# Transposes of the finished rows three steps behind their normalisation instead of one, in a graph network's second gather stage

## The chip, the cores and the metric

One NeuronCore of a Trainium2 chip runs the whole program. The metric is the device time of one execution in microseconds; the kernel before takes 3145.21 us as the median of three runs (3142.08 to 3146.8). "GpSimd" is POOL in the rows, "VectorE" DVE, "ScalarE" ACT, "TensorE" PE (PEld its weight loads), and "SyncE" SP; a q behind a name is that engine's sequencer or queue.

## The reference

Two layers of a graph network over 6250 nodes of 256 features and 100000 edges that are sorted by their destination. The part around the change is the second layer's message passing and linear attention:

```python
xn = _layernorm(x, axis=-1)
x = x + _L1_gnn_ref(xn, ...) + _L1_mix_ref(xn[None], ...)[0]
x = x + _L1_ffn_ref(_layernorm(x, axis=-1)[None], ...)[0]

# in _L1_gnn_ref
src = node_in[edge_src]
...
msg_rad = h @ fc_w2 / np.float32(np.sqrt(64.0))
messages = msg_ang * msg_rad
agg = jax.ops.segment_sum(messages, edge_dst, num_segments=node_in.shape[0])
```

The x after the second line is called x3 in the kernel; its layer norm, f3, is the input of the last feed-forward layer. That layer chooses its two experts for all rows at once, from the mean of f3 over the nodes.

## The kernel before, in words

The program is a row of phases; phase "g2" is the second gather stage, from about 1700 to 2735 us of the execution. Its time is laid out in steps by `timeline`: each engine has a list of plans, a plan being the steps at which the items of a kind begin and, for each function on them, how many steps later it runs. Each engine issues its instructions in the order of the steps and, in one step, in the order of the plans. A step is only an order and takes no time of its own; semaphores (`Steps`, `Landing`) make an engine wait for the others.

- **Groups** (`GROUPS`, 391 of them, one a step). A group is 2 x 128 edges. At its step GpSimd gathers their source rows from DRAM with two indirect DMAs (`gather`, L2484), into a buffer of 13 groups. One step later VectorE builds the one-hot matrix of destinations and half of its weighted copies (`make_hot`, L598 and L2119), three steps later ScalarE the other half (`weigh`, L2533). Five steps later TensorE sums the messages by destination (`sums`, L2131) into one of four PSUM banks, and seven steps later VectorE adds the bank to a ring of sums in SBUF (`accumulate`, L2614). The place in the ring is data, so ahead of each addition VectorE's sequencer loads it into a register (L2606).
- **Tiles** (`P9`, 50 tiles of 125 nodes, their steps at least 3 apart, in the last third of the stage). SyncE loads the tile's transposed rows xmT (L2459) and its x2 (L2463) at its step. VectorE adds the bias to x2 three steps later (`add_bias`, L2669); four steps later TensorE multiplies the rows and the finished ring columns with the weights (`product`, L2773 and L2778); five steps later VectorE adds up x3 (`x3_of`, L2677 and L2679) and takes its row statistics (L1442 to L1448). SyncE stores x3 at six steps (L2467). ScalarE clears ring columns for a later tile once a product has read them (`zero`, L2497).
- **Finished rows** (`F3`, for each pair of tiles 12 and 15 steps after the pair's second). VectorE normalises x3 to f3 (`f3_of`, L1457); SyncE stores it one step later (L2471). TensorE transposes it (`turned`, L2785) into the single bank TURN, ScalarE copies the transpose out to f3T, with the sums over nodes that the last layer needs (`copy`, L2524), and SyncE stores f3T (L2475). f3 and f3T have four buffers each.
- **Radial weights** (`RAD`, `CHUNKS`) for the edges are made along the way: L2715 and L2727 on TensorE, L2545 on ScalarE, L2589 and L2595 on VectorE.

In TensorE's order of one step the sums come first, then the radial work, then `turned`, then `product`. The tile's functions with the waits that tie the two engines are these:

```python
def product(i):
    ...
    sums3.wait(e, i - 1, "x3")
def turned(i):
    ln.norm.wait(e, i, "f")
    copied.wait(e, i - 1, "c1")
def x3_of(i):
    r = i % XR
    rows.wait(e, i, "rows")
```

Of the kernel before, what the change touches and what calls it, by code (L numbers as in the profile page):

```python
# [136 lines left out]
def gps_kernel(nc, A, out):  # L137
# [55 lines left out]
    with top:  # L193
# [2109 lines left out]
        with Phase("g2") as ph:  # L2303
# [121 lines left out]
            with nc.Block() as block:  # L2425
                @block.sync
                def _(e):
                    for to, src in ((rel[:, :, :].rearrange("p g j -> p (g j)"), rel_d), (base[:, :], base_d)):
                        e.dma_start(to, src).then_inc(s_in, 16)
                    def load_emb(n):  # L2430
                        eturn.wait(e, NV * (n - 1) - 1, "turn")
                        load_chunk(e, emb, n, e_in)
                    load_emb(1)
                    e.dma_start(w2r[:, :], A["L1_gnn_fc_w2"].rearrange("c a -> (a c)").partition_broadcast(P)).then_inc(s_w2r, 16)
                    e.dma_start(wkv[:, :, :], chunked(A["L1_mix_WkvT"])).then_inc(s_w, 16)
                    e.wait_ge(s_wz, 1)
                    for u in range(UU):
                        e.dma_start(w1b[u * K1:(u + 1) * K1, u, :], A["L1_gnn_fc_w1"]).then_inc(s_wb, 16)

                    def load_kv(i):  # L2440
                        proj.wait(e, i - 2, "v")
                        k_in.start(e.dma_start(kT[:, i % 2, :, :],
                                               xmT_d[i // 2].rearrange("p (c t n) -> p c t n", c=DC, t=2)[:, :, i % 2, :]),
                                   i % 2)

                    off = e.value_load(own_row[0:1, 0:1], min_val=0, max_val=N)

                    def load_rest(i):
                        e.dma_start(wq[:, :, :], chunked(A["L1_mix_Wq"])).then_inc(s_c, 16)
                        e.dma_start(wo[:, :, :], chunked(A["L1_mix_WoutT"])).then_inc(s_c, 16)  # L2450
                        e.dma_start(f3[:, 0, :], A["L1_mix_bout"].partition_broadcast(TN)).then_inc(s_c, 16)
                        e.dma_start(rwt[:, :, :], chunked(A["L1_ffn_Wr"])).then_inc(s_head, 16)
                        e.dma_start(br[:, :], A["L1_ffn_br"].rearrange("(a n) -> a n", a=1)).then_inc(s_head, 16)

                    def load(i):
                        if i == 0:
                            dots.wait(e, NT - 1, "dots")
                        rows.wait(e, i - XI, "rows")
                        x_in.start(e.dma_start(xmT[:, i % XI, :, :],  # L2459
                                               xmT_d[i // 2].rearrange("p (c t n) -> p c t n", c=DC, t=2)[:, :, i % 2, :]),  # L2460
                                   i % XI)
                        biased.wait(e, i - XI, "xb")
                        x_in.start(e.dma_start(x2[:, i % XI, :], xm_d[ds(off + i * TN, TN), :]), i % XI)  # L2463

                    def store_x3(i):
                        sums3.wait(e, i, "x3")
                        x_out.start(e.dma_start(tile_of(x3_d, i), x3[:, i % XR, :]), i % XR)  # L2467

                    def store_f3(i):
                        ln.norm.wait(e, i, "f")  # L2470
                        f_out.start(e.dma_start(tile_of(f3_d, i), f3[:, i % FR, :]), i % FR)  # L2471

                    def store_f3T(i):
                        copied.wait(e, i, "c1")
                        t_out.start(e.dma_start(f3T_d[i], f3T[:, i % FR, :, :].rearrange("p c n -> p (c n)")), i % FR)  # L2475
                    timeline(LAST_STEP, (CHUNKS[:-1], [(lambda i: load_emb(i + 2), 2)]), (KV, [(load_kv, 0)]), ([FIRST], [(load_rest, 0)]),
                             (P9, [(load, 0), (store_x3, 6)]), (F3, [(store_f3, 1), (store_f3T, 4)]))
                @block.gpsimd
                def _(e):
                    def gather(g):  # L2480
# [9 lines left out]
                @block.scalar  # L2490
                def _(e):
                    def zero(b):
                        rows.wait(e, b - RB, "rows")
                        to = ring[:, :, cols(b)]
                        pads = [ring[:, :, RING1:RING1 + WIN]] if b % RB == 0 else []
                        for part in (*pads, to):
                            ins = e.activation(part, iota[:, 0:1].unsqueeze(2).broadcast_to([P, SL, part.shape[2]]), ACT.Copy)  # L2497
                        blank.done(ins, "zero")

                    def square(i):  # L2500
                        sizes.wait(e, i - 1, "sum")
                        dots.wait(e, i - 2, "dots")
                        for q, bank, to, name, copy in ((0, KB, k1, "k", "raw"), (H1, V, v1, "v", "copy")):
                            proj.wait(e, i, name)
                            squares.done(e.activation(sq[:, q:q + H1, :].rearrange("p h d -> p (h d)"), ps[0:TN, bank, :],
                                                      ACT.Square), name)
                            squares.done(e.activation(to[:, i % 2, :], ps[0:TN, bank, :], ACT.Copy), copy)

                    def roots(i):
                        sizes.wait(e, i, "prod")  # L2510
                        kn.wait(e, i - 2, "k")
                        kroot.done(e.activation(rs[:, i % 2, :], pr[:, i % 2, :], ACT.Sqrt), "root")

                    def deviations(i):
                        ln.stats.wait(e, 2 * i + 1, "pre")
                        ln.norm.wait(e, 2 * i + 1 - XR, "f")
                        at = slice(2 * i % XR, 2 * i % XR + 2)
                        spread_of.done(e.activation(ln.rs[:, at, 0], ln.pre[:, at, 0], ACT.Sqrt), "dev")

                    def copy(i):  # L2520
                        turn.wait(e, i, "turn")
                        t_out.wait(e, i % FR, i // FR - 1)
                        for c in range(DC):
                            copied.done(e.activation(f3T[:, i % FR, c, :], ps[:, TURN, c * TN:(c + 1) * TN], ACT.Copy,  # L2524
                                                     accum_out=fsum[:, c, i:i + 1]), f"c{c}")
                    def weigh(g):
                        u, n, k = g % HR, g // (P // 2), 2 * g % P + 1
                        ready.wait(e, g, "hot")
                        scaled.wait(e, n - 1, "wr")
                        summed.wait(e, g - HR, "sums")  # L2530
                        w = WINS[g]
                        for m in range(4):
                            ins = e.activation(hotw[:, u, 1, m * w:(m + 1) * w], hot[:, u, 1, 0:w], ACT.Copy,  # L2533
                                               scale=chunk(n)[:, k, m:m + 1])
                        ready1.done(ins, "hotw")

                    def copy_emb(i):
                        eturn.wait(e, i, "turn")
                        hidden.wait(e, i - 2, "hid")
                        ecopy.done(e.activation(embT[:, i % 2, :], ps[0:UU * K1, 2, 0:P], ACT.Copy), "embT")  # L2540

                    def do_silu(i):
                        hidden.wait(e, i, "hid")
                        rads.wait(e, i - 2, "mul")
                        silu.done(e.activation(hs[:, i % 2, :, :],  # L2545
                                               ps[:, 7, 0:UU * C1].rearrange("p (u c) -> p u c", u=UU),
                                               ACT.Silu, scale=K1 ** -0.5), "silu")
                    timeline(LAST_STEP, (GROUPS, [(weigh, 3)]), (RAD, [(do_silu, 7), (copy_emb, 3)]), (ZERO, [(zero, 0)]),
                             (KV, [(square, 5), (roots, 8)]), (PAIRS, [(deviations, 9)]), (F3, [(copy, 2)]))

                @block.vector
                def _(e):
# [147 lines left out]
                def _(e):  # L2700
# [80 lines left out]
# [3 lines that stand above are left out]
                        for c in range(DC):  # L2784
# [1 line left out]
                                             ident[0:TN, 0:TN])  # L2786
                        turn.done(mm, "turn")
                    timeline(LAST_STEP, (GROUPS, [(sums, LEAD)]), (RAD, [(hidden_of, 5), (turn_emb, 1)]), (CHUNKS, [(turn_radial, 11)]),
                             (KV, [(products, 11), (project, 3)]), (MIX, [(mix_wo, 1), (mix_wq, 3)]), (F3, [(turned, 1)]),
                             (P9, [(product, 4)]))  # L2790


# [263 lines left out]
```

## Time and profile before

| | |
|---|---|
| median of 3 runs | 3145.21 us (3142.08 to 3146.8) |
| the profiled execution | 3143.74 us |
| its span | 3142.1 us |
| mean granted TensorE clock | 0.942 of full speed |
| TensorE busy, matmuls | 2647.7 us (84%) |
| VectorE busy | 1739.7 us (55%) |
| ScalarE busy | 1429.4 us (45%) |
| GpSimd busy | 1809.6 us (58%) |

The profile is of one execution. Its span is what lies between the first and the last instruction. A busy share over the whole span says little of this stage: each phase has another limit, and the sequencer's own instructions (register loads, semaphores, the issue of a DMA) count as idle time. The row of a wait names the instruction that waited and the one whose end released it.

### The profile page before, as it was taken

To read this page: it belongs to the slowest core of one execution; us is meant where nothing else is said; L and a number is where in the kernel's file an instruction comes from. 1 tells how busy PE (TensorE), PEld (TensorE's weight loads), DVE (VectorE), ACT (ScalarE), POOL (GpSimd) and SP (SyncE) were. 2 spreads that over 40 slices of the span, in tenths; PEclk is the share of its full clock that TensorE was granted. 3 is DMA by queue.
4 is the path that set the end of the run, shared out by engine and by line. 5 is a ranking of instruction groups with operands and counts; after the bars stand their busy time and mean duration, and the time that the engine had idled before them with its cause. 6 is when DMAs were issued, how large, how long until landed. Compare 5 with 4: busy or idle time off the path is not lost. (4 is left out here: it accounts for less than half of the span.)

```text
span 3142.1 us, 54187 instructions
## 1 busy us (share of the span) xinstructions
PE 2647.7 (84%) x14909; PEld 2219.0 (71%) x14909; DVE 1739.7 (55%) x5390; ACT 1429.4 (45%) x3996; POOL 1809.6 (58%) x1962
## 2 busy tenths in 40 slices
PE   1999998898988998699933899999887888689998
PEld 1877778777887886688832666666676677578886
DVE  7733336787776567333355556566566667533333
ACT  4022222442222553233346988788566766322221
POOL 5777777767773355344476777777777777200000
PEclk9999999999999998899965999999999999899999
DMA  7364446667673774333367444444466655422222
GB/s 224 113 190 144 136 140 200 222 198 219 216 220 123 215 237 146 103 95 95 92 186 233 116 125 117 125 117 128 121 181 177 176 162 161 123 76 72 70 65 55
DMA packets 291700, 464.77 MB, mean 148 GB/s; under 512 B 91221, under 2 KB 224276, under 8 KB 290074
## 3 DMA queue, kind: packets, MB, share of 16 engines
q1 hardware_dynamic: 207804, 232.37, 25.2%
q0 software_dynamic: 81216, 221.98, 24.0%
q10 hardware_dynamic: 2402, 7.19, 0.7%
q8 instruction: 115, 1.88, 0.2%
q14 instruction: 163, 1.34, 0.1%
HBM read 349.16 MB, written 112.23 MB: 147 GB/s over the span
## 5 line engine op out<-in xcount | busy, mean ns | idle before, releaser
L2484 POOL DMA_INDIRECT g_got<-xm_d,idx x782 | 757.4, 969 | 253.6 <-issue 219.4
L876 POOL DMA_INDIRECT g_got<-xn_d,idx x702 | 680.4, 969 | 240.5 <-issue 211.3
L2131 PEld LDWEIGHTS ps<-g_hotw,g_got 128*128 128x128 f32 x3128 | 402.3, 196 | 161.6 <-issue 81.3
L2131 PE MATMUL ps<-g_hotw,g_got 128*128 128x128 f32 (+11 forms) x3128 | 423.0, 285 | 91.0 <-DMA g_got<-xm_d,idx 59.9
L1261 PEld LDWEIGHTS ps<-g_hot,g_got 128*128 128x128 f32 x2808 | 357.5, 196 | 80.4 <-DMA g_got<-xn_d,idx 37.7
L1261 PE MATMUL ps<-g_hot,g_got 128*128 128x120 f32 (+4 forms) x2808 | 372.2, 280 | 36.4 <-DMA g_got<-xn_d,idx 25.7
L2533 ACT ACTIVATE g_hotw<-g_hot,g_wr 128x16 f32<-128x16 f32 (+8 forms) x1308 | 300.8, 309 | 90.8 <-DVE g_hot L598 90.2
L1453 POOL TENSOR_TENSOR p_ln_rs<-p_ln_pre,neg_half 125x2 f32<-125x2 f32 x50 | 35.2, 704 | 518.2 <-DVE p_ln_pre L1448 518.2
L2614 DVE TENSOR_TENSOR g_ring<-g_ring,ps 128x84 f32 (+10 forms) x391 | 133.4, 341 | 305.9 <-PE ps L2131 155.8
L2047 POOL DMA_INDIRECT z_d<-p_yj,p_to x108 | 121.9, 1128 | 205.1 <-DVE p_to L2080 183.3
L2934 ACT ACTIVATE p_hid<-ps,p_b 128x250 f32<-128x250 f32 x200 | 82.9, 466 | 278.6 <-PE ps L2896 278.6
L2011 PE MATMUL ps<-gin_hid,p_wj 128*128 128x256 f32 x864 | 197.4, 382 | 1.1 <-ACT gin_hid L1953 0.8
L1662 PE MATMUL ps<-gin_w,gin_hid 128*125 128x256 f32 x800 | 190.4, 388 | 9.1 <-POOL p_before L1721 9.1
L2913 PE MATMUL ps<-p_w,p_hid 128*125 128x256 f32 x800 | 179.2, 382 | 22.2 <-ACT p_hid L2934 22.2
L1393 PE MATMUL ps<-g_hT,g_w 128*128 128x250 f32 x800 | 191.9, 384 | 0.8 <-DVE g_hT L1084 0.8
L1072 DVE TENSOR_TENSOR g_ring<-g_ring,ps 128x40 f32 (+9 forms) x351 | 74.0, 211 | 208.7 <-PE ps L1261 125.7
L2896 PE MATMUL ps<-p_f3T,p_w 128*128 128x250 f32 x800 | 175.3, 375 | 13.3 <-DMA p_w<-in_L_ffn_W 13.3
L2913 PEld LDWEIGHTS ps<-p_w,p_hid 128*125 128x125 f32 x800 | 148.2, 188 | 52.9 <-ACT p_hid L2934 30.2
L2737 PE MATMUL ps<-g_half 128*125 128x512 f32 x400 | 184.9, 605 | 0.0
L2011 PEld LDWEIGHTS ps<-gin_hid,p_wj 128*128 128x128 f32 x864 | 165.1, 191 | 24.4 <-issue 1.1
L1962 ACT ACTIVATE gin_hid<-ps,p_wj 128x256 f32<-128x256 f32 x216 | 90.7, 471 | 188.6 <-PE ps L2011 188.6
L2896 PEld LDWEIGHTS ps<-p_f3T,p_w 128*128 128x128 f32 x800 | 151.6, 190 | 33.1 <-issue 13.4
(376 smaller groups left out, 5042.3 us busy)
## 6 DMA issues: line engine op xcount, KB each, us to landing
h_d<-gin_hid SPq DMA_DIRECT2D x23, 1000.0 KB, 7.8
gin_hid<-h_d SPq DMA_DIRECT2D x23, 1000.0 KB
p_xr<-jobs_d SPq DMA_DIRECT2D x54, 258.0 KB, 2.9
g_got<-xm_d,idx POOLq DMA_INDIRECT x782
g_half<-xmT_d SPq DMA_DIRECT2D x100, 125.0 KB
g_got<-xn_d,idx POOLq DMA_INDIRECT x702
p_wj<-z_d SPq DMA_DIRECT2D x50, 224.0 KB
q_d<-g_qo SPq DMA_DIRECT2D x25, 250.0 KB
```

The source lines that it names most:

```text
L876: landed.start(e.indirect_dma_start(got[:, k % (2 * GB), :], None, xn_d[0:N, :], bass.IndirectOffsetOnAxis(ap=idx[:, HT + k:HT + k + 1], a ...
L1261: mm = e.matmul(to, got[:, 2 * (g % GB) + j, c * P:(c + 1) * P], hot[:, g % HR, j, 0:w].unsqueeze(1).broadcast_to([P, r, w]), start=(j == ...
L1393: mm = e.matmul(ps[:, 5 + n % 2, k * BN:(k + 1) * BN], w1[:, c, f:f + P], hT[:, i % 2, c, :], start=(c == 0), stop=(c == DC - 1))
L1662: mm = e.matmul(ps[0:TN, i % 2, t * D:(t + 1) * D], hid[:, slot(i), c, t * TN:(t + 1) * TN], w2[:, c, :], start=(c == 0), stop=(c == HC - 1))
L2011: mm = e.matmul(ps[:, 2 * k + u, o * JOB:(o + 1) * JOB], w[:, c, o * P:(o + 1) * P], src[:, u, c, :], start=(c == 0), stop=(c == DC - 1))
L2131: mm = e.matmul(to, rows[j][:, c * P:(c + 1) * P], hotw[:, j, c * w:4 * w].unsqueeze(1).broadcast_to([P, r, n]), start=(j == 0), stop=(j = ...
L2484: landed.start(e.indirect_dma_start(got[:, 2 * (g % GB) + j, :], None, xm_d[0:N, :], bass.IndirectOffsetOnAxis(ap=idx[:, 2 * g + j:2 * g + ...
L2533: ins = e.activation(hotw[:, u, 1, m * w:(m + 1) * w], hot[:, u, 1, 0:w], ACT.Copy, scale=chunk(n)[:, k, m:m + 1])
L2614: added.done(e.tensor_tensor(to, to, sums_of(bank_of(g)[0], w, bank_of(g)[1]), ALU.add), "add")
L2737: mm = e.matmul(ps[0:TN, bank, :], kT[:, i % 2, c, :], wkv[:, c, at:at + INNER], start=(c == 0), stop=(c == DC - 1))
L2896: mm = e.matmul(ps[:, q, m * BN:(m + 1) * BN], w1[:, k, c, f * P:(f + 1) * P], f3T[:, u, :, c * TN:(c + 1) * TN], start=(c == 0), stop=(c ...
L2913: mm = e.matmul(ps[0:TN, 4 + u, t * D:(t + 1) * D], hid[:, u, k, f, t * TN:(t + 1) * TN], w2[:, k, f, :], start=(j == 0), stop=(j == 2 * F ...
```

## The change

Three numbers of plans are changed, all on `F3`. TensorE's transposes `turned` go from one to three steps after the normalisation, ScalarE's `copy` from two to four, and SyncE's `store_f3T` from four to six. What they compute and their counts stay.

```diff
@@ SyncE
-                             (P9, [(load, 0), (store_x3, 6)]), (F3, [(store_f3, 1), (store_f3T, 4)]))
+                             (P9, [(load, 0), (store_x3, 6)]), (F3, [(store_f3, 1), (store_f3T, 6)]))
@@ ScalarE
-                             (KV, [(square, 5), (roots, 8)]), (PAIRS, [(deviations, 9)]), (F3, [(copy, 2)]))
+                             (KV, [(square, 5), (roots, 8)]), (PAIRS, [(deviations, 9)]), (F3, [(copy, 4)]))
@@ TensorE
-                             (KV, [(products, 11), (project, 3)]), (MIX, [(mix_wo, 1), (mix_wq, 3)]), (F3, [(turned, 1)]),
+                             (KV, [(products, 11), (project, 3)]), (MIX, [(mix_wo, 1), (mix_wq, 3)]), (F3, [(turned, 3)]),
```

**TensorE, where a tile comes every third step.** The rows are the transposes (L2785), the product (L2773, L2778) and the sums of groups (two rows of L2131 each). Before:

```order
L2785 MATMUL ps<-ident,g_f 128x125 x2
L2773 MATMUL ps<-g_mix,g_half 125x256 x2
L2778 MATMUL ps<-wm,g_ring 125x128 x2
L2778 MATMUL ps<-wm,g_ring 125x64 x2
L2778 MATMUL ps<-wm,g_ring 125x128
L2778 MATMUL ps<-wm,g_ring 125x64 x2
L2131 MATMUL ps<-g_hotw,g_got 128x128 x2
L2131 MATMUL ps<-g_hotw,g_got 128x96 x2
L2131 MATMUL ps<-g_hotw,g_got 128x128 x2
L2131 MATMUL ps<-g_hotw,g_got 128x96 x2
L2131 MATMUL ps<-g_hotw,g_got 128x128 x2
L2131 MATMUL ps<-g_hotw,g_got 128x96 x2
```

Now:

```order
L2785 MATMUL ps<-ident,g_f 128x125 x2
L2131 MATMUL ps<-g_hotw,g_got 128x128 x2
L2131 MATMUL ps<-g_hotw,g_got 128x96 x2
L2727 MATMUL ps<-g_w1b,g_embT 128x512
L2773 MATMUL ps<-g_mix,g_half 125x256 x2
L2778 MATMUL ps<-wm,g_ring 125x128 x2
L2778 MATMUL ps<-wm,g_ring 125x64 x2
L2778 MATMUL ps<-wm,g_ring 125x128
L2778 MATMUL ps<-wm,g_ring 125x64 x2
L2131 MATMUL ps<-g_hotw,g_got 128x128 x2
L2131 MATMUL ps<-g_hotw,g_got 128x96 x2
L2131 MATMUL ps<-g_hotw,g_got 128x128 x2
```

The transposes stood directly ahead of a product; now the sums of one group follow them, and the product comes behind those. Of the 50 products, 30 stand directly behind transposes before, and 3 now.

**TensorE, at the stage's end.** The last sums and the last two products. Before:

```order
L2785 MATMUL ps<-ident,g_f 128x125 x2
L2131 MATMUL ps<-g_hotw,g_got 128x176 x2
L2131 MATMUL ps<-g_hotw,g_got 128x132 x2
L2785 MATMUL ps<-ident,g_f 128x125 x2
L2773 MATMUL ps<-g_mix,g_half 125x256 x2
L2778 MATMUL ps<-wm,g_ring 125x128 x2
L2778 MATMUL ps<-wm,g_ring 125x64 x2
L2778 MATMUL ps<-wm,g_ring 125x128
L2778 MATMUL ps<-wm,g_ring 125x64 x2
L2773 MATMUL ps<-g_mix,g_half 125x256 x2
```

Now:

```order
L2131 MATMUL ps<-g_hotw,g_got 128x176 x2
L2131 MATMUL ps<-g_hotw,g_got 128x132 x2
L2785 MATMUL ps<-ident,g_f 128x125 x2
L2773 MATMUL ps<-g_mix,g_half 125x256 x2
L2778 MATMUL ps<-wm,g_ring 125x128 x2
L2778 MATMUL ps<-wm,g_ring 125x64 x2
L2778 MATMUL ps<-wm,g_ring 125x128
L2778 MATMUL ps<-wm,g_ring 125x64 x2
L2785 MATMUL ps<-ident,g_f 128x125 x2
L2773 MATMUL ps<-g_mix,g_half 125x256 x2
```

Before, transposes stand directly ahead of the last product but one. Now those are of an earlier tile, and the transposes that stood there come behind that product.

**SyncE, where a tile comes every third step.** The stores are of x3 (x_d, L2467), f3 (f_d, L2471) and f3T (L2475), the loads xmT (L2459) and x2 (L2463). Before:

```order
L2471 DMA f_d<-g_f 125x256
L2475 DMA f3T_d<-g_f3T 128x250
L2459 DMA g_half<-xmT_d 128x2x125
L2463 ISA
L2463 DMA g_half<-xm_d 125x256
L2467 DMA x_d<-g_half 125x256
L2471 DMA f_d<-g_f 125x256
```

Now:

```order
L2467 DMA x_d<-g_half 125x256
L2475 DMA f3T_d<-g_f3T 128x250
L2471 DMA f_d<-g_f 125x256
L2459 DMA g_half<-xmT_d 128x2x125
L2463 ISA
L2463 DMA g_half<-xm_d 125x256
L2467 DMA x_d<-g_half 125x256
L2475 DMA f3T_d<-g_f3T 128x250
```

The store of f3T went out behind that of the next tile's f3; now it goes out behind that of x3. It stands behind f3's in 37 of 46 rows of SyncE's order before and in 12 of 49 now, and behind x3's in 8 before and 31 now. GpSimd's and VectorE's orders are the same in both kernels. (ISA is a register instruction of SyncE for the address of x2.)

## Rows read from the trace of the kernel before

**Rows 1.** The gathers of L2484: count, duration ns min/median/max, first and last start.
```profile
L2484 POOL DMA_INDIRECT g_got<-xm_d,idx x782: 942/946/2625, 1703.0 to 2697.3; - x196
```

**Rows 2.** Chain, then timeline (start us, us, what): a landing; last gather; last sums.
```profile
2303.15 5.08 DMA g_got<-xm_d,idx
...
2697.29 1.06 POOL L2484 DMA_INDIRECT g_got<-xm_d,idx  x1 [0.30 <-issue]
...
2717.91 1.21 PE L2131 MATMUL ps<-g_hotw,g_got 128*128 128x176 f32 x8
```

**Rows 3.** A stretch, its length, busy us of PE, PEld, DVE, ACT, POOL, clock, DMA.
```profile
2400.00:2500.00 100.00, 80.97 (x534) 69.69 (x532) 67.82 (x209) 70.95 (x239) 75.93 (x80) 0.93 0.63 175
```

**Rows 4.** Waits from 2280 to 2740 us: us in total, times, longest.
```profile
DVE g_ring L2614 <- issue: 80.9, 104, 2.0
...
PE ps L2785 <- DVE g_f L1457: 49.8, 33, 3.2
...
DVE g_half L2677 <- PE ps L2778: 13.8, 11, 2.5
```

**Rows 5.** VectorE's sequencer loads, 1900 to 2200, then 2300 to 2700 us.
```profile
L2606 DVEq TENSOR_LOAD <-g_base x119: 297/303/321, 1899.9 to 2198.9; - x119
...
L2606 DVEq TENSOR_LOAD <-g_base x150: 298/315/1705, 2300.9 to 2697.1; - x150
```

**Rows 6.** Timeline of one cycle, 2359 to 2367 us; in brackets the idle time before.
```profile
2359.02 0.15 DVE L1448 TENSOR_SCALAR g_ln_pre<-g_ln_mv 125x1 f32<-125x1 f32 x1
...
2361.13 0.39 DVE L2614 TENSOR_TENSOR g_ring<-g_ring,ps 128x224 f32 x1 [1.96 <-issue]
...
2362.09 0.41 DVE L1457 TENSOR_SCALAR g_f<-g_half,g_ln_mv,g_ln_rs 125x256 f32<-125x256 f32 x1
...
2362.55 0.68 PE L2785 MATMUL ps<-ident,g_f 125*128 125x125 f32 x2 [3.07 <-DVE g_f L1457]
...
2362.83 0.36 SPq L2475 DMA_DIRECT2D f3T_d<-g_f3T  x1
...
2363.59 0.29 DVE L2119 TENSOR_TENSOR g_hotw<-g_hot,g_wr 128x128 f32<-128x128 f32 x1
...
2365.57 0.39 DVE L2614 TENSOR_TENSOR g_ring<-g_ring,ps 128x224 f32 x1 [1.68 <-issue]
...
2366.94 0.28 DVE L2677 SCALAR_TENSOR_TENSOR g_half<-ps,xm_mv,g_half 125x64 f32<-125x64 f32 x1 [0.52 <-PE ps L2778]
```

**Rows 7.** Timeline of the stage's end, from 2721 us.
```profile
2721.30 0.43 PE L2785 MATMUL ps<-ident,g_f 125*128 125x125 f32 x2 [2.18 <-DVE g_f L1457]
...
2724.11 0.28 DVE L2677 SCALAR_TENSOR_TENSOR g_half<-ps,xm_mv,g_half 125x64 f32<-125x64 f32 x1 [2.09 <-PE ps L2778]
...
2727.49 0.28 DVE L2677 SCALAR_TENSOR_TENSOR g_half<-ps,xm_mv,g_half 125x64 f32<-125x64 f32 x1 [0.85 <-PE ps L2778]
```

**Rows 8.** VectorE's waits from 2300 to 2700 us.
```profile
DVE g_half L2677 <- PE ps L2778: 8.8, 7, 2.5
```

**Rows 9.** Timeline, 2308 to 2316 us: late data, then the longest wait of L2677.
```profile
2308.27 2.00 PE L2131 MATMUL ps<-g_hotw,g_got 128*128 128x112 f32 x8 [2.12 <-DMA g_got<-xm_d,idx]
...
2315.96 0.28 DVE L2677 SCALAR_TENSOR_TENSOR g_half<-ps,xm_mv,g_half 125x64 f32<-125x64 f32 x1 [2.47 <-PE ps L2778]
```

**Rows 10.** Timeline from 2542 us: a burst behind f3 without f3T.
```profile
2542.08 0.33 DVE L2119 TENSOR_TENSOR g_hotw<-g_hot,g_wr 128x160 f32<-128x160 f32 x1
...
2543.44 0.45 DVE L2614 TENSOR_TENSOR g_ring<-g_ring,ps 128x280 f32 x1 [0.65 <-issue]
```

**Rows 11.** Timeline from 2647 us: f3T's store between x3's and the next load.
```profile
2647.22 0.26 SPq L2467 DMA_DIRECT2D x_d<-g_half  x1
...
2647.52 0.36 SPq L2475 DMA_DIRECT2D f3T_d<-g_f3T  x1
...
2648.01 0.15 DVE L1448 TENSOR_SCALAR g_ln_pre<-g_ln_mv 125x1 f32<-125x1 f32 x1
...
2649.34 0.48 DVE L2614 TENSOR_TENSOR g_ring<-g_ring,ps 128x308 f32 x1 [1.17 <-issue]
```

## The prediction

> **What bounds the kernel now.** The edit lives in the second gather stage, so I first look at who paces it. The gathers of L2484 run from 1703.0 to 2697.3 us, 782 of them [rows 1]: (2697.3 - 1703.0) / 781 = 1.27 us each, two to a step, so 2.55 us a step. GpSimd's idle time is the short gap it takes between any two, so up to 2697 the gathers set the pace. But the stage does not end with them. The last gather starts at 2697.29 and takes 1.06 us; a gather's data reaches TensorE 5.08 us after it where nothing is behind; that would be 2703.4, yet the sums of the last group start at 2717.91 [rows 2]. So 14.5 us of backlog stand behind the gathers at their end, and whatever holds TensorE and VectorE back while the rows are finished (2280 to 2740 us) is paid there.
>
> Next, which of the two engines made the backlog. In 100 us of that stretch TensorE is busy 80.97 and VectorE 67.82 [rows 3], which points to TensorE. The waits say the reverse. TensorE waited 49.8 us in 33 pieces for the normalised rows f3 of VectorE (L2785 behind L1457); VectorE waited for finished products only 13.8 us in 11 pieces (L2677 behind L2778), and its other idle time, 80.9 us ahead of the ring additions of L2614, has "issue" as its end [rows 4]. That issue time is VectorE's own sequencer, which reads the ring position of a group by a load (L2606) ahead of each addition. In the quiet part of the stage that load never takes over 321 ns; here it takes up to 1705 [rows 5]. So VectorE with its sequencer is the chain, TensorE is the one that waits, and **the 49.8 us are not for sale**: a wait taken from TensorE is worth what it takes from VectorE's waits.
>
> **The tie between them** is seen in one cycle [rows 6]. VectorE makes f3 of one tile at 2362.09; TensorE has stood 3.07 us for it, turns it at 2362.55, and only then runs the product of the newest tile (before: 30 of the 50 products stand right behind a transpose in TensorE's order; after: 3). The product is done as VectorE's L2677 starts at 2366.94, after a wait of 0.52 us. From the transposes to L2677 are 4.39 us; for the same work at the stage's end they are 2724.11 - 2721.30 = 2.81 [rows 7], so the stop was followed by a slow stretch. The mean granted clock around it is 0.93 [rows 3]: part of the time stands at 1.2 instead of 2.4 GHz.
>
> **The change, term by term**, against the profiled execution (3143.74 us; the median of the runs, 3145.21, stands 1.5 above it). Nothing is added or removed. VectorE's and GpSimd's orders are the same, row for row.
>
> *Transposes three steps behind.* TensorE reaches the transposes two steps later, some 5 us at 2.55 a step; the longest stop it has now is 3.2 us [rows 4], so f3 is there. The product of that step no longer has the f3 stop, nor the transposes, ahead of it. How much of VectorE's wait goes:
> - 2300 to 2700: 8.8 us in 7 waits [rows 8]. The largest, 2.47 us at 2315.96, was not made by f3: TensorE had stood 2.12 us for gathered data at 2308.27 [rows 9], and will again. I leave it in; the other six are 8.8 - 2.47 = 6.3 us, all behind products that a transpose precedes. Gain 6.3 (bounds 3 and 8.8).
> - after 2700: 13.8 - 8.8 = 5.0 us. Of these, 0.85 us is the last product's, which starts on the row sums of the product before it and keeps its wait. The wait of 2.09 us at 2724.11 goes: TensorE stood 2.18 us for f3 until 2721.30 ahead of that product, though the last sums were done at 2719.1 (2717.91 + 1.21) [rows 7]. It comes behind the last gather, so it counts one for one. The other 5.0 - 0.85 - 2.09 = 2.1 us likewise. Gain 4.2 (bounds 2 and 4.2).
>
> *What replaces the stop.* Freed, TensorE runs ahead until the next sums need a bank whose addition VectorE has not done: four banks, additions seven steps behind their gather against five for the sums, so it can be two steps ahead and not more. It will stand there; nobody waits for it then. Its earlier sums free gather buffers earlier, which gathers that run back to back do not need. Cost 0.
>
> *Copies on ScalarE, two steps later*: 100 copies, unchanged, still one step behind their transposes. The buffer is four tiles deep and a tile comes at most every third step, so a slot is copied into again 12 steps on at the earliest; its store follows the copy by two steps, as before, and 10 steps are left for it to land. Cost 0.
>
> *Stores of f3T on SyncE, two steps later.* SyncE's queue is in order. Now the store goes out right behind the store of the next f3 (37 of the 46 rows of it in SyncE's order), followed by the loads; afterwards mostly right behind the store of x3 (31 of 49 rows), and in 12 behind f3. This matters for the long loads of L2606. In the cycle shown, f3T's store goes at 2362.83, and from the row at 2363.59 to the ring addition at 2365.57 are 1.98 us [rows 6]. Where the burst held no f3T, the same two rows are 2543.44 - 2542.08 = 1.36 apart [rows 10]: 0.62 less. Behind row statistics the store of x3 alone gave 2361.13 - 2359.02 = 2.11 [rows 6], x3 with f3T 2649.34 - 2648.01 = 1.33 [rows 11], so an f3T there costs nothing that these rows show. For 37 - 12 = 25 tiles: between 25 x 0.62 = 15.5 us gained and, were the second place to answer as the first does, nothing. That loads wait for transfers at all is my reading of a coincidence, and the same kinds of burst differ by 0.8 us, so I take a third of the way to the gain: 4.5 us.
>
> *Tail.* The last four transposes stand behind the last product in both orders: 0.
>
> Sum: 6.3 + 4.2 + 4.5 = 15.0 us. Of it 6.3 + 2.1 + 4.5 = 12.9 fall before the last sums, within the 14.5 us of backlog; all of the backlog and the 2.09 at the end would be 16.6. So 3143.7 - 15.0 = 3128.7 on the profiled run, 3130.2 as a median. **I predict 3130 us.** Without the load term, 3134.7; with everything at its upper bound the cap of the backlog gives 3128.6.
>
> **Rivals.**
> *A, VectorE's waits come back.* If TensorE only stops elsewhere, and its products still end late, the gain shrinks to 0 to 4 us. For it: all of TensorE's idle time remains, since VectorE sets the pace, and it is now taken at the bank waits. Against it: a product then starts two VectorE steps, some 5 us, ahead of its reader, and even at 4.39 us it is done. Time: 3142 to 3145. The Trainium skill (TensorE: Matmul & The Clock Gate, the part on the HAM clock gate) has a rule on this side: an array that stood idle runs at half its clock until it has been busy again. By that rule moving a stop does not cure a slow stretch, and where one stop of 3 us becomes a longer one it makes more of them; the 4.39 against 2.81 us above agree with it.
>
> *B, slower: the second burst.* The f3T store joins x3's, just ahead of the load that follows the row statistics, and there is such a load for every tile. That load is on the chain. If it always went from the short case to the long one of my rows (1.33 to 2.11, 0.78 us), half of that as a mean over the 50 tiles is 19.5 us; with 10.5 gained and no relief behind f3: 3145.2 + 9.0 = 3154. It decides from 10.5 / 50 = 0.21 us per tile on. Against it: the two rows stand the wrong way round for it.
>
> *C, TensorE was the bound after all*: busy share 81%. Then the 49.8 us pull away all backlog there is: 14.5 + 2.1 = 16.6, so 3128.6 as a median. Against it: VectorE's waits for it are a quarter of the reverse.
>
> **How the numbers follow.** No change here means within 0.2%, 6.3 us, which is about what a measurement of this kernel can tell apart. Forecast 0.68, C 0.08, A 0.18, B 0.06. The forecast's own range is 3125 to 3138: both waits at their bounds, the load term from 0 to the cap, 2 us of scatter between runs. To hold 8 in 10 it must reach into A: 3123 to 3142. Faster: the forecast nearly whole (below 3138.9), C, and little of A: 0.78. Same: most of A, the end of the forecast, a part of B: 0.17. Slower by over 6.3 us: 0.05.
>
> **What would show it.** Right: in the new profile TensorE's wait at L2785 falls from 49.8 us to under 10, and TensorE waits by tens of us more at L2131 behind L2614; L2677's 13.8 us fall to some 4 (2.5 and 0.85 stay); idle time "issue" ahead of L2614 falls by some 4; gathers still end near 2697, and the last sums come at about 2705 instead of 2717.9. Wrong: L2677's waits as large as before (A), "issue" ahead of L2614 grown by 10 us or more (B), or a last gather later than 2699, which I have no term for.

## The result and the profile after

The changed kernel takes 3131.71 us as the median of five runs (3124.7 to 3144.05), against 3145.21 (3142.08 to 3146.8) before. The ratio is 0.9963, with a 95% interval of 0.9947 to 0.9979: by this ratio it is 11.6 us faster (between 6.6 and 16.7; the two medians lie 13.5 apart), a small gain that is clear of the noise. Its runs lie 19 us apart, more than the first ones of the kernel before; its profiled execution took 3133.81 us.

The page of the changed kernel, its span and the first line of part 1 (busy us, share, instructions):

```profile
span 3132.2 us, 54187 instructions
...
PE 2653.0 (85%) x14909; PEld 2221.0 (71%) x14909; DVE 1737.8 (55%) x5390; ACT 1430.2 (46%) x3996; POOL 1815.6 (58%) x1962
```

TensorE's busy time is 2653.0 us, and was 2647.7: nothing was saved on it. The gathers of the stage (columns as in [rows 1]):

```profile
L2484 POOL DMA_INDIRECT g_got<-xm_d,idx x782: 942/946/2247, 1705.4 to 2702.9; - x196
```

They begin 2.4 us later than in [rows 1] and end 5.6 us later, at 1.277 us each instead of 1.273. The edit touches neither the work ahead of the stage nor the gathers' own instructions. In the traces of before, this kernel and three of the experiments below (all but same_step of those on chip 9), the 782 gathers take 994.3 to 1000.5 us from the first start to the last, 994.6 in two_steps, which is half of this change. So this profiled run lost some 3 us to the pace of its gathers, for which the forecast had no term; whether the edit has a part in it is not shown.

The waits of the changed kernel from 2280 to 2740 us (us in total, times, longest), to be held against [rows 4]:

```profile
DVE g_ring L2614 <- issue: 76.0, 105, 2.2
...
DVE g_ring L2614 <- PE ps L2131: 30.9, 33, 1.6
PE ps L2131 <- DVE g_ring L2614: 30.6, 23, 3.0
PE ps L2131 <- DVE g_hot L598: 25.0, 26, 3.4
ACT g_ring L2497 <- PE ps L2778: 23.0, 15, 3.2
...
DVE g_half L2677 <- PE ps L2778: 5.3, 3, 3.0
...
PE ps L2785 <- DVE g_f L1457: 2.3, 1, 2.3
```

TensorE's wait for f3, 49.8 us, is down to 2.3 (one wait, in the tail). In its place stand 30.6 us for ring additions (15.0 before) and 25.0 for one-hot matrices (8.6 before), both made by VectorE. Most of TensorE's idle time is still there, in other places: from 2280 us to the end of its last sums it is idle 71.9 us of 432.0, where it was 80.1 of 439.1. VectorE's wait for products fell from 13.8 us to 5.3. ScalarE, whose clearing of ring columns also waits for products, shows the same, with 23.0 us where it had 65.5.

The timeline of one cycle, answering to [rows 6] (start, us, line, and in brackets the idle time before):

```profile
2362.84 0.41 DVE L1457 TENSOR_SCALAR g_f<-g_half,g_ln_mv,g_ln_rs 125x256 f32<-125x256 f32 x1
...
2364.28 1.10 PE L2131 MATMUL ps<-g_hotw,g_got 128*128 128x128 f32 x8 [0.76 <-DVE g_hot L598]
...
2365.22 0.38 PE L2785 MATMUL ps<-ident,g_f 125*128 125x125 f32 x2
...
2366.66 0.28 DVE L2677 SCALAR_TENSOR_TENSOR g_half<-ps,xm_mv,g_half 125x64 f32<-125x64 f32 x1
...
2367.47 1.04 PE L2773 MATMUL ps<-g_mix,g_half 128*125 128x256 f32 x4
...
2368.35 1.64 PE L2778 MATMUL ps<-wm,g_ring 128*125 128x128 f32 x14
...
2370.37 0.41 DVE L1457 TENSOR_SCALAR g_f<-g_half,g_ln_mv,g_ln_rs 125x256 f32<-125x256 f32 x1
```

f3 is made at 2362.84. TensorE does not wait for it: it sums a group, then turns at 2365.22. VectorE reads the finished product of the tile before at 2366.66 with no idle time, and TensorE starts the next product (L2773) at 2367.47, before VectorE has even made the next f3 (2370.37). From one f3 to the next are 7.5 us here.

The end of the stage, answering to [rows 2] and [rows 7]:

```profile
2702.87 0.96 POOL L2484 DMA_INDIRECT g_got<-xm_d,idx  x1 [0.30 <-issue]
...
2709.65 2.31 PE L2131 MATMUL ps<-g_hotw,g_got 128*128 128x176 f32 x16
...
2711.80 0.38 PE L2785 MATMUL ps<-ident,g_f 125*128 125x125 f32 x2
...
2712.01 1.03 PE L2773 MATMUL ps<-g_mix,g_half 128*125 128x256 f32 x4
...
2714.56 0.43 PE L2785 MATMUL ps<-ident,g_f 125*128 125x125 f32 x2
...
2715.20 0.28 DVE L2677 SCALAR_TENSOR_TENSOR g_half<-ps,xm_mv,g_half 125x64 f32<-125x64 f32 x1
...
2716.01 1.13 PE L2773 MATMUL ps<-g_mix,g_half 128*125 128x256 f32 x4 [1.01 <-DMA g_half<-xm_d]
...
2718.65 0.28 DVE L2677 SCALAR_TENSOR_TENSOR g_half<-ps,xm_mv,g_half 125x64 f32<-125x64 f32 x1 [0.92 <-PE ps L2778]
```

The last sums (two groups in one row) end at 2711.96, 9.1 us after the start of the last gather; before, they ended at 2719.12, 21.8 us after it. The backlog is 12.7 us shorter. Since the gathers took 3.2 us longer, the stretch from the first gather's start to the end of the last sums is shorter by less: 1006.6 us against 1016.1, 9.5 us. I call this stretch the stage's length below. The last product but one (2712.01) has a transpose of 0.38 us ahead of it and no stop, and its reader at 2715.20 has no idle time where 2.09 us stood. The last reader waits 0.92 us (0.85 before), and its product now 1.01 us for its loaded rows, a small new wait.

The sequencer's loads from 2300 to 2700 us, as in [rows 5]:

```profile
L2606 DVEq TENSOR_LOAD <-g_base x154: 299/318/1964, 2300.7 to 2699.4; - x154
```

Median and longest did not fall: 318 and 1964 ns against 315 and 1705.

### The profile page after: what moved, and what is told of

It is laid out like the page before. It is cut to its first block and busy times, and to the rows that moved or that the text cites. A ratio compares the mean times of both kernels' runs of the same rounds, so it can differ in the third digit from the quotient of the medians.

```text
span 3132.2 us, 54187 instructions
## 1 busy us (share of the span) xinstructions
PE 2653.0 (85%) x14909; PEld 2221.0 (71%) x14909; DVE 1737.8 (55%) x5390; ACT 1430.2 (46%) x3996; POOL 1815.6 (58%) x1962
## 5 line engine op out<-in xcount | busy, mean ns | idle before, releaser
L2484 POOL DMA_INDIRECT g_got<-xm_d,idx x782 | 760.5, 973 | 253.4 <-issue 221.8
L2131 PEld LDWEIGHTS ps<-g_hotw,g_got 128*128 128x128 f32 x3128 | 406.7, 198 | 199.8 <-issue 117.8
L2131 PE MATMUL ps<-g_hotw,g_got 128*128 128x128 f32 (+11 forms) x3128 | 432.7, 288 | 125.0 <-DMA g_got<-xm_d,idx 62.2
L2614 DVE TENSOR_TENSOR g_ring<-g_ring,ps 128x84 f32 (+10 forms) x391 | 133.5, 341 | 303.6 <-PE ps L2131 155.3
L2896 PEld LDWEIGHTS ps<-p_f3T,p_w 128*128 128x128 f32 x800 | 151.3, 189 | 32.2 <-issue 12.5
```

What stands on the lines that cost most here:

```text
L2131: mm = e.matmul(to, rows[j][:, c * P:(c + 1) * P], hotw[:, j, c * w:4 * w].unsqueeze(1).broadcast_to([P, r, n]), start=(j == 0), stop=(j = ...
L2484: landed.start(e.indirect_dma_start(got[:, 2 * (g % GB) + j, :], None, xm_d[0:N, :], bass.IndirectOffsetOnAxis(ap=idx[:, 2 * g + j:2 * g + ...
L2614: added.done(e.tensor_tensor(to, to, sums_of(bank_of(g)[0], w, bank_of(g)[1]), ALU.add), "add")
L2896: mm = e.matmul(ps[:, q, m * BN:(m + 1) * BN], w1[:, k, c, f * P:(f + 1) * P], f3T[:, u, :, c * TN:(c + 1) * TN], start=(c == 0), stop=(c ...
```

## The experiments

Two theories were set against each other. **The tie**: VectorE with its sequencer is the chain of this part of the stage, and the change gains what VectorE had to wait for products that stood behind the f3 stop. **The stores**: the gain is in SyncE's order, through the sequencer's loads. Nine kernels ran, three of them on two chips and the changed one again, on three chips. Chips 14 and 4 ran every kernel some 13% slower than the chip of the result (before: 3560.07 and 3562.46 us), so only ratios to the kernel before on the same chip are compared. No trace of the kernel before was taken there; waits are held against those of store_late.

### The changed kernel again (chip 14)

> The changed kernel itself, for the scale of the others. If the gain of 0.37% stands, 3126 to 3140 us. Theory of the tie (VectorE waited for products that stood behind the f3 stop): L2677's wait from 2280 to 2740 us is again near 5 us where it was 13.8, and the last sums come before 2713 us. Rival of the stores (the gain is in SyncE's order and the sequencer loads L2606): L2677's wait may be anything, and the longest loads behind f3 are shorter. If runs differ by several us, as the first five did, the gathers' own pace should show it: a last gather between 2697 and 2704 us.

3550.13 us, ratio 0.9969 (0.9952 to 0.9987). The ratio stands on a second chip; the expected microseconds do not, since the whole chip was slower. One sign of it is seen in its timeline:

```profile
2717.81 0.27 PE L2785 MATMUL ps<-ident,g_f 125*128 125x125 f32 x1 [1.09 <-issue]
...
2718.53 0.27 PE L2785 MATMUL ps<-ident,g_f 125*128 125x125 f32 x1 [0.45 <-issue]
...
2719.36 0.28 DVE L2677 SCALAR_TENSOR_TENSOR g_half<-ps,xm_mv,g_half 125x64 f32<-125x64 f32 x1 [5.03 <-remote]
```

The two transposes of one tile, one row of two in the timelines above, are 0.72 us apart, with idle time "issue" between them though neither waits for anything, and VectorE then stands 5.03 us for the product; the profile names the releaser "remote". On these chips TensorE itself is often late, so VectorE's waits for products are larger (76.4 us "remote" and 6.8 for TensorE, where some 5 were expected) and partly of another kind. The mean granted clock in the traces of chips 14 and 4 is 0.893 to 0.905, against 0.941 here.

The limit of the stage is another one there too. Its gathers stood idle, in all and by releaser (us, times):

```profile
  PE ps L2131: 127.5, 68
  DMA g_own<-xn_d: 110.0, 48
```

In the trace of the result the first of these was 16.2 us and the second did not occur. The 782 gathers take 1198.6 us here, 1.53 us each. So on chips 14 and 4 the gathers do not set the pace, and their ratios say which edits bring the gain, but not that VectorE is the chain.

### Only the store later (chips 14 and 4)

```diff
-(F3, [(store_f3, 1), (store_f3T, 4)])
+(F3, [(store_f3, 1), (store_f3T, 6)])
```

> Only SyncE's store of f3T goes two steps later; transposes and copies stay where they were. Theory of the tie: nothing that TensorE or VectorE wait for changes, L2677's wait stays at 12 to 15 us, and the time is that of before within 3 us (3142 to 3148). Rival of the stores: at least half of the gain is here, 3135 to 3140 us, with the idle time (issue) ahead of L2614 down by 5 us or more from 80.9.

> Again only the store of f3T two steps later, since the first chip ran all kernels 13% slower, with late instructions on TensorE. Theory of the tie: within 0.1% of before, L2677's wait near 13.8 us. Rival of the stores, now from its row: the burst behind f3 is shorter and idle time (issue) ahead of L2614 falls by 4 us or more, ratio 0.998 to 0.9985.

Ratios 1.0004 (0.9986 to 1.0021) and 1.0007 (0.9989 to 1.0025): no gain, twice. The stops of TensorE at L2785, matmuls and weight loads added up, and below them those of VectorE at L2677, on chip 14 (us, times):

```profile
  DVE g_f L1457: 78.7, 39
  issue: 51.4, 39
```

```profile
  remote: 58.7, 22
  PE ps L2778: 31.5, 15
```

The expected 12 to 15 us at L2677 do not hold on these chips: the two rows make 90.2 us here and 101.2 on chip 4.

### Transposes and copies later, the store in its old place (chips 14 and 4)

```diff
-(F3, [(copy, 2)])
+(F3, [(copy, 4)])
-(F3, [(turned, 1)])
+(F3, [(turned, 3)])
```

> Transposes and copies go two steps later as in the change, the store of f3T stays four steps behind the normalisation, in the step of its copy. Theory of the tie: all of the gain, 3128 to 3138 us, L2677's wait near 5 us, and the burst of stores behind f3 as before the change. Rival of the stores: 3140 to 3146 us. Rival of a stopped queue: SyncE waits for the copy with the next tile's loads behind it; then TensorE waits at L2773 for xmT and the time is above 3146 us.

> Again transposes and copies late, the store in its old place. Theory of the tie: ratio 0.9955 to 0.9975, as the whole change, L2677's wait 4 to 8 us. If the stores brought part of the change's gain, this has less than the change.

Ratios 0.9961 (0.994 to 0.9981) and 0.9967 (0.9952 to 0.9982), the whole gain both times. VectorE's idle time at L2677, chip 14:

```profile
  remote: 77.5, 25
  PE ps L2778: 3.7, 3
```

Together 81.2 us against 90.2 with only the store moved; what is named as TensorE's product fell from 31.5 to 3.7. On chip 4 the sum is 62.2 us against 101.2, where 4 to 8 were expected. The named part fell as the theory says, but the sum does not follow the gain: it fell by 9.0 us on one chip and 39.0 on the other, for nearly the same ratio. SyncE's queue was not stopped to any effect.

### The product ahead of the transposes in a step (chips 14 and 4)

```diff
-(MIX, [(mix_wo, 1), (mix_wq, 3)]), (F3, [(turned, 1)]),
-(P9, [(product, 4)]))
+(MIX, [(mix_wo, 1), (mix_wq, 3)]),
+(P9, [(product, 4)]), (F3, [(turned, 1)]))
```

> The kernel before with one edit: in TensorE's order of a step the product comes ahead of the transposes; the transposes still stand one step behind the normalisation. Theory of the tie in its narrow form (what cost time was the product behind the f3 stop, not the stop): the f3 wait stays at 30 us or more, L2677's wait falls to 3 to 7 us, and the time is 3130 to 3139 us. Wide form (each stop of TensorE costs, since it holds up sums as well): less than half of the gain, 3139 to 3145 us. Rival of the stores: 3142 to 3147.

> Again the kernel before with the product ahead of the transposes in a step. It had three quarters of the gain on the slow chip. Narrow theory: 0.9965 to 0.998, L2677's wait 4 to 8 us, while TensorE still waits over 25 us for f3, which then costs next to nothing. Wide theory: 0.998 to 1.0.

Ratios 0.9976 (0.9959 to 0.9994) and 0.997 (0.9953 to 0.9987). Nothing is moved to another step; two plans have changed places. The stops at L2785 and those at L2677, chip 14:

```profile
  DVE g_f L1457: 27.9, 27
  issue: 9.9, 11
```

```profile
  remote: 80.9, 24
  PE ps L2778: 7.7, 5
```

Most of the gain (0.24% where the whole change and its variant had 0.31 and 0.39% on chip 14, 0.30% beside 0.33% on chip 4) is had by the order inside a step alone. The expected sign of the narrow form did not come, though: TensorE's matmuls at L2785 were to wait 30 us or more for f3 (over 25 on chip 4), and they waited 11.2 and 5.6 us, where store_late had 34.5 and 42.1, since TensorE comes to f3 later by a product. VectorE's stops at L2677 make 88.6 us in all, against 90.2, of which the part named as TensorE's product fell from 31.5 to 7.7. So this edit took away the product behind the stop and most of the stop as well, and on a chip where TensorE holds the gathers back it cannot tell the narrow form from the wide one. Whether the remainder to the full change is real, the intervals do not say.

### Half the dose, and the other way (chip 9)

> Transposes two steps behind the normalisation instead of one, copies three, stores of f3T five: half of the change. Theory of the tie: what counts is that a product no longer stands directly behind a transpose that waits for f3, and that TensorE may be two steps ahead of VectorE anyway; both are had at two steps, so the whole gain of the change is here (ratio to the kernel before 0.996 to 0.998, L2677's wait as small as in the change). Rival of dose (each step of slack frees some of TensorE's stops): half of it, 0.998 to 0.999.

> The other way: transposes in the very step of the normalisation, copies one step later, stores of f3T three. The suspected cost doubled. Theory of the tie: TensorE may now not pass the step that VectorE is in, each product and each group's sums behind a transpose are later by up to a step, L2677's wait grows to twice that of before or more, and the time rises by 0.3 to 1.5%. Rival of the stores, or that TensorE's stops cost nothing: within 0.1% of before.

`turned`, `copy` and `store_f3T` at 2, 3 and 5 give 0.9968 (0.9954 to 0.9981) with a median of 3136.41 us; at 0, 1 and 3 they give 1.0144 (1.0124 to 1.0164), 3194.47 us. This chip ran the kernel before in 3145.29 us, so its microseconds compare with those of the result. The waits of two_steps from 2280 to 2740 us:

```profile
DVE g_half L2677 <- PE ps L2778: 8.2, 5, 3.4
...
PE ps L2785 <- DVE g_f L1457: 2.9, 4, 1.8
```

and those of same_step from 2280 to 2780 us:

```profile
PE ps L2785 <- DVE g_f L1457: 95.4, 40, 5.2
...
DVE g_half L2677 <- PE ps L2778: 73.8, 39, 4.0
POOL g_got L2484 <- PE ps L2131: 54.4, 56, 3.8
```

Two steps bring the gain of three within the intervals: half of the gain would be about 0.9982, just outside the interval, so the dose rival (0.998 to 0.999) is all but excluded. The stage's length says the same: 1006.9 us, against 1006.6 with the whole change. With the transposes in the step of the normalisation VectorE's wait for products is 73.8 us instead of 13.8, 60.0 more, TensorE's wait for f3 is 45.6 us more, and the kernel is 49 us slower; the stage's length is 1065.8 us, 49.7 more. The backlog now reached the gathers themselves, which stood 54.4 us for free buffers (11.9 before) and take 1034.7 us from first to last, 40.4 more. Both waits grew by about what the time did, so this run shows that the tie costs time, not which of the two waits the time follows.

### The ring position loaded early (chip 9)

```diff
+places = {}
+
+def place_of(g):
+    return e.value_load(base[0:1, g:g + 1], min_val=0, max_val=RING1 - 1)
 def accumulate(g):
-    at = e.value_load(base[0:1, g:g + 1], min_val=0, max_val=RING1 - 1)
+    at = places.pop(g) if g in places else place_of(g)
...
     added.done(e.tensor_tensor(to, to, sums_of(bank_of(g)[0], w, bank_of(g)[1]), ALU.add), "add")
+    if ALONE <= g < NG - 1:
+        places[g + 1] = place_of(g + 1)
```

> The changed kernel, with one edit more: in the last part of the stage VectorE's sequencer loads the ring position of the next group right behind the dispatch of a ring addition, instead of ahead of its own addition. It so runs beside the addition, and not behind the row statistics, where the store of x3 has just gone out. Theory that VectorE with its sequencer is the chain there: the idle time (issue) ahead of the ring additions falls by 20 us or more, the backlog behind the gathers that the change left (some 4 us over a landing) goes, and the time is 0.1 to 0.25% under that of the changed kernel, no more, since the gathers set the pace. Rival (TensorE or the gathers alone bound what is left): the same as the changed kernel within 0.05%.

> The kernel before with the early load of the ring position, transposes one step behind as before. If VectorE's chain of loads made the backlog, and the f3 stops of TensorE only passed it on, this alone brings as much as the change did, ratio 0.995 to 0.998, and TensorE's wait for f3 falls below 30 us from 49.8. If the backlog comes from the tie, whatever VectorE's pace, it brings less than half of that.

On the changed kernel: 3127.95 us (3122.28 to 3130.12), ratio 0.9934 (0.9916 to 0.9952), the fastest of all that ran and by the two ratios 0.29% under the changed kernel, a little more than the 0.1 to 0.25% expected. On the kernel before: 3134.86 us, ratio 0.9955 (0.9938 to 0.9973). Waits of the first, from 2280 to 2740 us (L2684 is L2677 of the other kernels):

```profile
PE ps L2131 <- DMA g_got<-xm_d,idx: 46.8, 40, 3.3
...
DVE g_half L2684 <- PE ps L2785: 34.3, 13, 6.6
DVE g_hot L598 <- issue: 32.2, 54, 1.5
```

The idle time ahead of the ring additions is gone as a group; in its place stand 32.2 us ahead of the one-hot matrices and 16.7 ahead of the radial work (L2589), 27 us less in sum than the 76.0 of the changed kernel. More telling is the first row: TensorE now waits 46.8 us for gathered data, where it waited 3.6 us before the change and 8.5 after it. The chain of VectorE has dropped behind the gathers, and the backlog is gone: the last sums end 7.6 us after the start of the last gather, and a gather of 1.06 us, a landing of 5.08 [rows 2] and a group's sums of 1.21 are 7.35. I take the 34.3 us that VectorE then waits for products to be waits for data, passed on; they are more than the 13.8 of before and cost nothing that the time shows.

The second kernel, from 2290 to 2750 us:

```profile
DVE g_half L2684 <- PE ps L2785: 37.7, 19, 6.9
...
PE ps L2131 <- DMA g_got<-xm_d,idx: 29.3, 17, 4.6
```

Here TensorE's f3 wait stays at 35.5 us of 49.8, over the 30 that I had set as a mark, and yet the last sums end 8.9 us after the start of the last gather, as with the change (9.1), not 21.8. The stage's length is 1009.4 us, 6.7 less than before, and by the ratio the time fell by some 14 us, as much as with the change within the intervals. So it is enough to shorten VectorE's chain, by its waits (the change) or by its sequencer's work (this edit), and most of TensorE's f3 stops may stay.

What both together add to one of them is less clear. By the medians it is much: 3127.95 us against 3134.86 for the early load alone (the two intervals overlap a little) and against 3136.41 for two_steps on the same chip (they do not). But the first gathers of early_place start earlier, before anything that the edit touches:

```profile
L2484 POOL DMA_INDIRECT g_got<-xm_d,idx x782: 942/947/2157, 1700.4 to 2699.1; - x196
```

They start at 1705.3 in two_steps. In the traced executions the stage's length is 1006.3 us, as with the change alone (1006.6), and the difference to two_steps is nearly all in that start. Where the medians' difference comes from stays open; the traces show no gain in the stage from doing both.

### Each f3T stored twice (chip 4)

```diff
+spare_d = scratch("spare_d", (2 * NB, P, DC * TN))
...
-t_out.start(e.dma_start(f3T_d[i], ...), i % FR)
+for to in (spare_d, f3T_d):
+    t_out.start(e.dma_start(to[i], ...), i % FR)
```

> The kernel before, with the suspected cost of the burst doubled: SyncE stores each f3T twice, first to a spare tensor in DRAM that nothing reads, then to its place. If the sequencer's loads L2606 are held up by transfers that have just been issued, the loads behind f3 grow (mean idle time ahead of L2614 up, 5 to 20 us in sum between 2280 and 2740 us) and the time rises by 0.1 to 0.6%, no more than that. If they are not, idle time and time stay within 0.1% of before.

Ratio 1.0016 (0.9996 to 1.0036), which holds both no change and the lower half of what was expected: inconclusive. Idle time "issue" ahead of the ring additions, over the whole stage, is 128.7 us against 125.2 with one late store on the same chip, below the 5 to 20 us more that were expected. The loads of the ring position from 2600 to 3100 us had a median of 349 ns and a maximum of 1494, against 314 and 1935 with one late store on the same chip. A cost of the second store is not shown, and up to 0.36% of the time is not excluded.

## Why the prediction was right

**The time.** 3130 us was forecast and 3131.71 measured, inside the range of 3123 to 3142, with "faster" at 0.78. The gain was 11.6 us by the ratio, for 15.0 in the sum. That the median came within 1.7 us is partly luck: the five runs lie 19 us apart, and 3134.7, the forecast without its load term, would have fitted as well. The profiled execution, for which the sum was made, was to take 3128.7 us and took 3133.81.

**What bounds the stage.** The mechanism fits what the traces show: of the 49.8 us of TensorE's wait 47.5 went, and 11.6 us were gained. Rival C, which sold them, cannot be told apart by its time of 3128.6, but it would have shown TensorE's other waits unchanged, while those at L2131 for VectorE grew from 15.0 + 8.6 to 30.6 + 25.0. Of this growth the prediction named only the ring additions, which were to grow by tens of us and grew by 15.6; the one-hot matrices, 16.4 us more, it did not foresee. early_place_before is the stronger evidence: the backlog goes with most of the f3 stops left in place. The full path, from the f3 stop over the late product to VectorE's wait, is read from the waits of two traces; no experiment on a fast chip took the product out from behind the stop and left the stop.

**The wait term.** 10.5 us were forecast (6.3 before 2700, 4.2 after it); L2677's wait fell by 13.8 - 5.3 = 8.5: by 4.4 before 2700 (8.8 to 4.4) and by 4.1 after it. In the tail the 2.09 us went as said. Before it, one wait of 3.04 us stands again where I left the one of 2.47, behind late data (TensorE stood 3.21 us for a gather until 2301.76) and the radial work on a slow TensorE: 1.99 us for the two matmuls of L2727 at 2303.55, where before such a pair took 0.90 at 2277.11 in the chain.

```profile
2303.55 1.99 PE L2727 MATMUL ps<-g_w1b,g_embT 80*128 80x512 f32 x2
...
2310.31 0.28 DVE L2677 SCALAR_TENSOR_TENSOR g_half<-ps,xm_mv,g_half 125x64 f32<-125x64 f32 x1 [3.04 <-PE ps L2778]
```

**The load term is the one that was mis-sized.** 4.5 us were forecast. VectorE's two idle groups ahead of L2614 fell from 80.9 + 29.5 to 76.0 + 30.9, by 3.5 us, and median and longest load did not fall. Added up over the timelines by the instruction ahead, the idle time fell almost only where a ring addition follows a one-hot matrix's copies (L2119), from 49.2 to 46.0 us at 63 places each; that is where the prediction put its relief, but the rows cannot say whether loads or sums brought it. With the stores moved alone there was no gain on two chips; but TensorE is late by itself on those, so they test VectorE's loads poorly. On a chip as fast as that of the result this part was not tried alone. I take it as 0 to 3.5 us, not shown. The reading of one pair of rows for a mean (0.62 us) was the weak step. The working has two slips as well. A third of 15.5 us is 5.2, not 4.5. And the forecast's own range of 3125 to 3138 does not come from its terms: both waits at their bounds, the load term from 0 to the cap and 2 us of scatter give 3126.6 to 3142.2. The wider range of 3123 to 3142 holds this to within 0.2 us.

**The backlog.** The last group's sums were to start at about 2705, with gathers ending near 2697; all sums had ended at 2712.0, with gathers ending at 2702.9. That is later than 2699, which the prediction had set as a sign of being wrong and had no term for; 2.4 us of it are the later start and 3.2 the slower gathers. From the last gather on, the shortening is 12.7 us, where 12.9 fell before the last sums in my sum, but that these agree is chance: 3.2 us of the 12.7 are the slower gathers. The stage's length fell by 9.5 us, which agrees with the two sizes above: 6.5 us of waits ahead of the tail and 3.5 of idle time, 10.0 in sum.

**The rivals.** A (waits come back elsewhere) fell: TensorE's did, VectorE's did not. The rule of the Trainium skill on the clock that A drew on (TensorE: Matmul & The Clock Gate, the part on the HAM clock gate) did not decide: from 2280 us to the last sums the mean granted clock is 0.94 after and 0.93 before, though the stops have changed places. (The 0.93 that the prediction read beside its cycle at 2362 us is that of 2400 to 2500; from 2300 to 2400 it is 0.91, which changes nothing in the reading.) B fell: from L1448, the end of the row statistics, to the ring addition that follows it are 1.28 us in the mean in both traces (45 places each), though f3T's store now mostly stands there.

## What to carry to other kernels

A long wait of an engine is worth what it makes the engine on the chain wait, so look for the few waits of the chain's own engine and ask what stood ahead of the work that it waited for. In an in-order queue, work that another engine is about to need had better not stand behind a wait for that same engine's newest result; here changing places inside a step brought most of the gain (on the two slower chips), and a third step of slack brought nothing over the second. The chain's own sequencer work (here a register load per step) is worth as much as its waits. Once the chain has dropped behind what feeds it, here the gathers, a second saving on it did not shorten the traced stage.

## What the runs showed of the hardware

The register loads of VectorE's sequencer take 296 to 330 ns in the quiet part of the stage (1900 to 2200 us, before and after) and up to 1964 ns from 2300 us on, where SyncE issues stores and loads; what lengthens them stayed open. Two chips ran the same program 13% slower (3560.07 and 3562.46 us against 3145.21 and 3145.29), with a mean granted clock of 0.893 to 0.905 against 0.94. In their traces TensorE stood between instructions that wait for nothing, as 0.72 us from one transpose to the next, where a pair as a whole otherwise took 0.38 to 0.68, and gathers waited for it. The gain in per cent was nearly the same on both kinds (0.31 and 0.37%), though not the same engine held the stage back.
